# One stage in place of four: local attention and gated MLP of two layers in one pipeline, the softmax's exponential taken head by head

## The chip, the cores and the metric

The kernel runs on one core of a Trainium2 chip. The core has TensorE (PE; its weight loads are PEld), VectorE (DVE), ScalarE (ACT), GpSimd (POOL) and SyncE (SP, which only issues DMAs here). Each runs its own list of instructions in order, and they meet by semaphores. The metric is the device time of one execution in microseconds (us), median of several runs.

## The reference, cut to what matters

The kernel computes four sub-layers on x of 4 sequences, 1024 tokens, width 128. The change is in the last one, two layers of windowed attention with a gated MLP:

```python
def _layer(x, wqkv, qs, ksc, wo, lg, lb, w1, b1, w2, b2):
    h = shift_token(x)                  # the upper 64 features come from the token before
    q, k, v = split(h @ wqkv, 3)        # 8 heads of 64
    q = l2norm(q) * qs; k = l2norm(k) * ksc
    q, k = rotary_xpos(q, k)
    o = local_attention(q, k, v)        # windows of 64: own window and the one before, softmax
    x = x + o @ wo
    h = shift_token(x)
    h = (h - mean(h)) / sqrt(var(h) + 1e-05) * lg + lb
    a, g = split(h @ w1 + b1, 2)        # 341 each
    x = x + (a * gelu(g)) @ w2 + b2
    return x
```

A sequence of the second layer needs all its own tokens of the first, but nothing of the other sequences.

## The kernel before

`STAGES` (L1805) lists nine stages, one after the other, with a barrier of all engines between them. Activations lie with features on partitions and the 4096 tokens along the free dimension (`x`, `branch`). The last five stages are `normalise` (a layer norm of x into `branch`, which also loads the attention's weights), then `attend` and `gated_mlp` for each layer.

`attend` (L1326) works in tiles of 128 tokens, 32 tiles for a layer. It is software pipelined by hand: in step g an engine does the projection of tile g, the norm of tile g - 1 (`NORM`), the scores of g - 3 (`SCORE`), the exponential of g - 4 (`EXP`), the transposed probabilities and their product with the values for g - 5 (`VALUE`), and the output projection of g - 6 (`OUT`). `steps` (L52) writes the first steps out and loops over the rest. Within a step the order on each engine is the order of the code.

- TensorE: eight transposes of the turned q and k (L1377), three projections of 128x512 (L1389), eight transposes of probabilities (L1399), mask and scores (L1411, L1425, L1430), output projection (L1443), values (L1464).
- ScalarE: copies of q, k out of PSUM (L1493, L1495), one Exp over all eight heads, 128x1024, in place in SBUF (L1500), Ln and Exp of the norms (L1505, L1508), copies L1513, L1515, L1516 and L1521, a Square (L1528), the copy L1534. It also makes the shifted input `hs` (L1485, L1486).
- VectorE: sum of squares (L1590), floor (L1594), the rotary products (L1601, L1608), the sum of the exponentials (L1615), its reciprocal (L1618), the row maximum (L1624), scores less maximum from PSUM to SBUF (L1628), the add to `branch` (L1635), the other half of `v_mix` (L1638).
- GpSimd: three elementwise operations of 128x1024 (L1550, L1555, L1564).

`gated_mlp` (L1656) first runs `layer_norm` over all tokens, then goes in chunks of 512 tokens, eight for a layer: six matmuls up (L1713), three Gelu on ScalarE (L1745), three gated products on VectorE (L1766), three matmuls down (L1722), and the add (L1772). Gelu and Exp lie in different tables of ScalarE; `preload_act_table_set` loads one at the start of a stage. The store of the result is issued chunk by chunk by SP.

Every matmul here is float32, and the profile shows each as two records.

## Time and profile before

| | us |
|---|---|
| median of 3 runs | 1866.24 (1866.13 to 1867.06) |
| the profiled execution | 1866.51 |
| its span, first to last instruction | 1864.7 |
| `attend`, first layer | 1036.3 to 1350.1: 313.8 |
| `layer_norm` and `gated_mlp`, first layer | 1350.1 to 1449.7: 99.6 |
| `attend`, second layer | 1449.7 to 1763.3: 313.6 |
| `layer_norm` and `gated_mlp`, second layer | 1763.3 to 1864.7: 101.4 |

Over the span PE is busy 78%, DVE 71%, ACT 57%, POOL 49%. These are means over nine stages with different limits; the four stages in the lower half of the table hold 828.4 us. A row of the timeline gives start, duration, engine, line and operation, and in brackets the idle time before it and who ended it. A duration ends when the result is out; on ScalarE and TensorE the next instruction starts some 0.1 to 0.2 us earlier, so that what an instruction costs its engine is the distance of two starts.

### The profile page before, as it was taken

Reading aid. Unit: us, or ns where it says so; the run is one execution under the profiler, and the core shown is the slowest. Engines: PE = TensorE matmul, PEld = TensorE weight load, DVE = VectorE, ACT = ScalarE, POOL = GpSimd, SP = SyncE. Lnnn points to the kernel's source line nnn. Section 1 sums busy time; section 2 is a strip of 40 time slices with the busy share of each in tenths; the row PEclk is TensorE's granted clock in tenths of the full one; section 3 lists DMA queues with packets and bytes.
Section 4 is the critical chain, followed back from the end, with each engine's and each line's share of the span. In section 5 each row is a group of like instructions: output and inputs, shape, how many; then the busy total and the mean of one; then the engine's idle time right before and its main releaser. Section 6 shows DMA issues by size and latency. Waiting matters only on the chain. (4 is left out here: it accounts for less than half of the span.)

```text
span 1864.7 us, 26805 instructions
## 1 busy us (share of the span) xinstructions
PE 1445.9 (78%) x8740; PEld 800.6 (43%) x8740; DVE 1316.6 (71%) x1932; ACT 1061.9 (57%) x1849; POOL 917.2 (49%) x468
## 2 busy tenths in 40 slices
PE   6755299667577777777679689999789689999789
PEld 2314288323122223222233256666634366666533
DVE  2954133266799999999721699999633699999534
ACT  4431155487656666566444677887542587887442
POOL 0431433103888988888500277767400466776300
PEclk8875599887799999999989899999979899999989
DMA  1007111300000000000001000000010000000001
GB/s 58 0 6 158 58 46 34 91 0 1 0 1 1 0 1 0 0 0 0 0 12 48 3 1 2 0 0 0 1 61 0 1 2 2 0 0 0 13 6 40
DMA packets 35020, 30.08 MB, mean 16 GB/s; under 512 B 7763, under 2 KB 29573, under 8 KB 34566
## 3 DMA queue, kind: packets, MB, share of 16 engines
q1 hardware_dynamic: 32646, 24.48, 5.0%
q0 software_dynamic: 2304, 4.74, 0.8%
q8 instruction: 35, 0.57, 0.1%
q14 instruction: 35, 0.29, 0.1%
HBM read 19.73 MB, written 9.47 MB: 16 GB/s over the span
## 5 line engine op out<-in xcount | busy, mean ns | idle before, releaser
L1550 POOL TENSOR_TENSOR at_direct<-at_direct,at_square 128x1024 f32<-128x1024 f32 x64 | 152.5, 2383 | 412.4 <-DVE at_square L1608 412.4
L1023 POOL TENSOR_TENSOR ssm_dbu<-ssm_dtu,ssm_b_all 128x1024 f32<-128x1024 f32 x128 | 298.5, 2360 | 21.6 <-ACT ssm_b_all L976 21.1
L884 PE MATMUL ssm_bank<-ssm_seen,ident 128*128 128x512 f32 x512 | 247.4, 606 | 45.1 <-POOL ssm_seen L1031 37.7
L971 ACT ACTIVATE ssm_bank<-ssm_dt,ssm_decay 128x512 f32<-128x512 f32 x256 | 176.8, 691 | 118.0 <-DVE ssm_state L1122 115.6
L1389 PE MATMUL at_ps<-at_wqkv,at_hs 128*128 128x512 f32 x384 | 187.9, 628 | 32.8 <-ACT at_hs L1486 17.6
L1122 DVE TENSOR_TENSOR_SCAN ssm_state<-ssm_bank,ssm_dbu 128x512 f32<-128x512 f32 x128 | 147.9, 1204 | 15.4 <-POOL ssm_dbu L1023 15.1
L1122 DVE TENSOR_TENSOR_SCAN ssm_state<-ssm_bank,ssm_carry,ssm_dbu 128x512 f32<-128x512 f32 x128 | 155.3, 1263 | 1.9 <-POOL ssm_dbu L1023 1.6
L884 PEld LDWEIGHTS ssm_bank<-ssm_seen,ident 128*128 128x128 f32 x512 | 95.8, 193 | 131.0 <-issue 63.9
L1555 POOL TENSOR_TENSOR at_prob<-at_prob,at_inv 128x1024 f32<-128x1024 f32 x64 | 121.4, 1897 | 21.8 <-DVE at_inv L1618 21.8
L1564 POOL TENSOR_TENSOR at_direct<-at_direct,at_rnorm 128x1024 f32<-128x1024 f32 x64 | 131.4, 2053 | 0.5
L1389 PEld LDWEIGHTS at_ps<-at_wqkv,at_hs 128*128 128x128 f32 x384 | 71.4, 199 | 108.0 <-issue 75.9
L1130 DVE TENSOR_TENSOR ssm_seen<-ssm_state,ssm_bank 128x1024 f32<-128x1024 f32 x96 | 114.5, 1193 | 0.0
L871 PE MATMUL ssm_bank<-ssm_parts,ssm_pick 128*128 (+1 forms) x128 | 50.0, 391 | 73.6 <-DVE ssm_seen L1130 73.5
L976 ACT ACTIVATE ssm_b_all<-ssm_bank 128x512 f32<-128x512 f32 x128 | 74.7, 584 | 47.2 <-PE ssm_bank L862 26.7
L1443 PE MATMUL at_ps<-at_oT,at_wo 128*128 128x128 f32 x512 | 73.6, 287 | 32.5 <-ACT at_v_mix L1516 31.1
L1590 DVE TENSOR_REDUCE at_sums<-at_square 128x16 f32<-128x1024 f32 x64 | 78.0, 1219 | 22.6 <-ACT at_square L1528 21.0
L1031 POOL TENSOR_TENSOR ssm_seen<-ssm_state,ssm_c_all 128x1024 f32<-128x1024 f32 x32 | 75.2, 2350 | 34.5 <-ACT ssm_c_all L980 34.5
L1713 PE MATMUL glu_bank<-glu_normed,glu_w 128*128 (+3 forms) x192 | 90.5, 625 | 1.7 <-DVE glu_w L1758 1.7
L1608 DVE TENSOR_TENSOR at_square<-at_qk,at_turn 128x256 f32<-128x256 f32 x256 | 90.7, 411 | 0.0
L1745 ACT ACTIVATE glu_gelu<-glu_bank,glu_b 128x512 f32<-128x512 f32 (+1 forms) x48 | 32.9, 685 | 92.6 <-PE glu_bank L1713 92.6
L1615 DVE TENSOR_REDUCE at_total<-at_prob 128x8 f32<-128x1024 f32 x64 | 77.2, 1206 | 9.0 <-ACT at_prob L1500 9.0
L1601 DVE TENSOR_TENSOR at_direct<-at_qk,at_turn 128x512 f32<-128x512 f32 x128 | 81.9, 678 | 0.0
(240 smaller groups left out, 3418.0 us busy)
## 6 DMA issues: line engine op xcount, KB each, us to landing
moe_w<-in_moe_w SPq DMA_DIRECT2D x16, 256.0 KB
moe_to_experts<-moe_empty SPq DMA_DIRECT2D x10, 258.0 KB, 8.0
moe_slot_rows<-moe_to_experts SPq DMA_DIRECT2D x10, 258.0 KB, 3.0
x<-in_x SPq DMA_DIRECT2D x8, 256.0 KB, 3.4
moe_rows<-moe_from_experts SPq DMA_DIRECT2D x8, 256.0 KB, 4.5
at_turn<-in_turn SPq DMA_DIRECT2D x2, 1024.0 KB
out_x<-x SPq DMA_DIRECT2D x8, 256.0 KB, 2.0
at_wqkv<-in_wqkv SPq DMA_DIRECT2D x2, 768.0 KB
```

Source lines behind the costliest of these rows:

```text
L884: last = nc.tensor.matmul(bank[Y0 + half][:], ident[:], seen[:, n % 2, half], start=n == 0, stop=False)
L971: nc.scalar.activation(bank[DA0 + half][:], dt[:, half, cols(b * 2 + k)], ACT.Exp, scale=decay[:, half, n:n + 1]).then_inc(s[f"da{half}"], 1)
L1023: nc.gpsimd.tensor_tensor(dbu[:, n % RING], dtu[:, k], b_all[:, n % 2:n % 2 + 1, :].broadcast_to([P, 2, CH]), ALU.mult).then_inc(s["dbu"], 1)
L1122: nc.vector.tensor_tensor_scan(state[:, n % RING, half], bank[DA0 + half][:], dbu[:, n % RING, half], start, ALU.mult, ALU.add).then_inc(s ...
L1130: nc.vector.tensor_tensor(seen[:, n % 2], state[:, n % RING], bank[C0][:].unsqueeze(1).broadcast_to([P, 2, CH]), ALU.mult).then_inc(s["see ...
L1389: last = nc.tensor.matmul(ps[:, to], hs[:, i * TILE:(i + 1) * TILE], w[:, m * INNER:(m + 1) * INNER], start=True, stop=True)
L1550: nc.gpsimd.tensor_tensor(direct[:, quarter], direct[:, quarter], crossed[:, half], ALU.add).then_inc(s["added"], 1)
L1555: nc.gpsimd.tensor_tensor(prob[:, half], prob[:, half], inv[:, half].unsqueeze(2).broadcast_to([P, HEADS, TILE]), ALU.mult).then_inc(s["we ...
L1564: nc.gpsimd.tensor_tensor(heads, heads, rnorm[:, half].unsqueeze(2).broadcast_to([P, 2 * HEADS, HEAD]), ALU.mult).then_inc(s["scaled"], 1)
L1601: nc.vector.tensor_tensor(to, of, turn[:, 0, at_tile, m:m + 1].broadcast_to([P, HEADS, HEAD]), ALU.mult)
L1608: last = nc.vector.tensor_tensor(to[:, :, h0:h0 + 32], of[:, :, h1:h1 + 32], turn[:, 1, at_tile, m:m + 1, h0:h0 + 32].broadcast_to([P, HEA ...
L1713: last = nc.tensor.matmul(bank[3 * m + c][0:size, :], w1[:, m * HID + first:m * HID + first + size], normed[:, cols(t)], start=True, stop= ...
```

## The change

The four stages become one, `ffn`, with steps g = 0 to 76 (`LAST`) over the 64 tiles of both layers; nothing in it is a loop of the machine, every step is written out. The tile's pipeline keeps its lags. In addition each chunk c of 512 tokens, once its four tiles have gone through the attention, has its MLP spread over seven steps: `chunk_at(g, 0)` is true in step 9 + 4c. A step so carries pieces of two chunks. I call a step kind 0, 1, 2 or 3 by (g - 9) mod 4, and bare where it has no piece of an MLP:

- kind 0: first two `values` of the chunk before, the output projection of the chunk (`to_rows`, four matmuls of 512 columns for four tiles together, two before and two after the scores);
- kind 1: the third `values` and two `down` of the chunk before, `centring`, a Square on ScalarE;
- kind 2: the third `down`, `variance`, then Ln and Exp (`root`), the normalised chunk on VectorE;
- kind 3: three `gates` on TensorE, a table load, three Gelu and a table load back on ScalarE.

Softmax: VectorE takes the row maximum as before and multiplies it by -1 (`lowered`); ScalarE takes the exponential from PSUM in eight instructions of 128x128, one for each head, with the negated maximum as bias and the row sum as a second output (`accum_out`). The subtraction (L1628) and the sum (L1615) on VectorE go. The scores' PSUM banks are held until the exponentials are done.

The token shifts (`hs`, `hs2`) and both halves of `v_mix` are now DMAs from SBUF to SBUF, issued by SP. The sum x + branch is on GpSimd. `normalise` loads the weights of both layers, the MLP's too, in 36 DMAs where it had 11.

```diff
-                if live(EXP):
-                    n, half = g - EXP, (i - EXP) % 2
-                    act.wait_ge(s["shifted"], done(n))
-                    nc.scalar.activation(prob[:, half], prob[:, half], ACT.Exp).then_inc(s["prob"], 1)
...
+LAST = PER_CHUNK * (ALL_CHUNKS - 1) + FIRST + 7
+HELD = 6
+TURNED = 3
...
+        def chunk_at(g, step):
+            c, phase = divmod(g - FIRST - step, PER_CHUNK)
+            return c if phase == 0 and 0 <= c < ALL_CHUNKS else None
...
+            def shift(q):
+                for c in range(q * CHUNKS, (q + 1) * CHUNKS):
+                    k = c % CHUNKS
+                    of = chunk_of(branch, c)
+                    sp.dma_start(hs[0:64, q % 2, k * CH:(k + 1) * CH], of[0:64]).then_inc(s["hs"], 16)
+                    sp.dma_start(hs[64:128, q % 2, 1 + k * CH:1 + (k + 1) * CH], of[64:128]).then_inc(s["hs"], 16)
...
+                c = chunk_at(g, 0)
+                if c is not None:
+                    sp.wait_ge(s["attended"], up_to(c))
+                    k, q = c % CHUNKS, c // CHUNKS
+                    if q >= 2:
+                        sp.wait_ge(s["centred"], up_to((q - 1) * CHUNKS - 1))
+                    of = chunk_of(branch, c)
+                    sp.wait_ge(s["hs2"], 32 * c)
+                    sp.dma_start(hs2[0:64, q % 2, k * CH:(k + 1) * CH], of[0:64]).then_inc(s["hs2"], 16)
+                    sp.dma_start(hs2[64:128, q % 2, 1 + k * CH:1 + (k + 1) * CH], of[64:128]).then_inc(s["hs2"], 16)
+                if real(g) and not opens(g):
+                    sp.wait_ge(s["v_copied"], up_to(g))
+                    if real(g - HELD):
+                        sp.wait_ge(s["av"], up_to(g - HELD))
+                    if real(g - 2):
+                        sp.wait_ge(mixed[g % 2], mixes(g - 2))
+                    sp.dma_start(v_mix[0:64, g % HELD], v[0:64, g % HELD]).then_inc(mixed[g % 2], 16)
+                    sp.dma_start(v_mix[64:128, g % HELD], v[64:128, (g - 1) % HELD]).then_inc(mixed[g % 2], 16)
...
+            for g in range(LAST + 1):
+                n = g - SCORE
...
+                if chunk_at(g, 4) is not None:
+                    values(chunk_at(g, 4), (0, 1))
+                if chunk_at(g, 0) is not None:
+                    to_rows(chunk_at(g, 0), (0, 1))
+                if chunk_at(g, 5) is not None:
+                    values(chunk_at(g, 5), (2,))
+                if chunk_at(g, 6) is not None:
+                    down(chunk_at(g, 6), (2,))
+                if chunk_at(g, 2) is not None:
+                    variance(chunk_at(g, 2))
+                if chunk_at(g, 3) is not None:
+                    gates(chunk_at(g, 3))
...
+                    nc.tensor.matmul(one[:], at, wqkv[:, g // PER_LAYER, 2 * INNER:], start=True, stop=True
+                                     ).then_inc(s["v_proj"], 1)
+                    if real(n):
+                        pe.wait_ge(s["kT_copied"], up_to(n))
...
+                if chunk_at(g, 5) is not None:
+                    down(chunk_at(g, 5), (0, 1))
+                if chunk_at(g, 0) is not None:
+                    to_rows(chunk_at(g, 0), (2, 3))
+                if chunk_at(g, 1) is not None:
+                    centring(chunk_at(g, 1))
...
+            def gelus(c):
+                act.preload_act_table_set("gelu_and_others")
+                if c >= 1:
+                    act.wait_ge(s["down"], up_to(c - 1))
+                for p, (first, size) in enumerate(HID_PARTS):
+                    act.wait_ge(s["gates"], c * PARTS_OF_HID + p + 1)
+                    nc.scalar.activation(hidden[0:size, p], glu[PART_BANK[p]][0:size, :], ACT.Gelu,
+                                         bias=b1[0:size, c // LAYER_CHUNKS, 1, p:p + 1]).then_inc(s["gelu"], 1)
+                act.preload_act_table_set("natural_log_exp_and_others")
...
+                n = g - EXP
+                if real(n):
+                    act.wait_ge(s["lowered"], up_to(n))
+                    if real(n - 2):
+                        act.wait_ge(s["pT"], up_to(n - 2))
+                        act.wait_ge(s["inv"], up_to(n - 2))
+                    for h in range(HEADS):
+                        last = nc.scalar.activation(prob[:, n % 2, h],
+                                                    scores[:, h // 4, h % 4 * TILE:(h % 4 + 1) * TILE], ACT.Exp,
+                                                    bias=peak[:, n % 2, h:h + 1], accum_out=total[:, n % 2, h:h + 1])
+                    last.then_inc(s["prob"], 1)
...
+                c = chunk_at(g, 2)
+                if c is not None and c >= LAYER_CHUNKS:
+                    pool.wait_ge(s["attended"], up_to(c))
+                    nc.gpsimd.tensor_tensor(chunk_of(x, c), chunk_of(x, c), chunk_of(branch, c), ALU.add
+                                            ).then_inc(s["summed"], 1)
...
+            def prods(c, parts):
+                for p in parts:
+                    size = HID_PARTS[p][1]
+                    dve.wait_ge(s["gelu"], c * PARTS_OF_HID + p + 1)
+                    dve.wait_ge(s["values"], c * PARTS_OF_HID + p + 1)
+                    nc.vector.scalar_tensor_tensor(hidden[0:size, p], glu[VALUE_BANK[p]][0:size, :],
+                                                   b1[0:size, c // LAYER_CHUNKS, 0, p:p + 1], hidden[0:size, p],
+                                                   ALU.add, ALU.mult).then_inc(s["prod"], 1)
...
+                n = g - SCORE
+                if real(n):
+                    dve.wait_ge(s["sim"], up_to(n))
+                    of = scores[:].rearrange("p a (h j) -> p (a h) j", h=4)
+                    nc.vector.tensor_reduce(peak[:, n % 2], of, AX_X, ALU.max).then_inc(s["peak"], 1)
+                    dve.wait_ge(s["peak"], up_to(n))
+                    nc.vector.tensor_scalar(peak[:, n % 2], peak[:, n % 2], -1.0, None, ALU.mult
+                                            ).then_inc(s["lowered"], 1)
...
+STAGES = [min_gru, experts, mamba, mlp, normalise, ffn]
```

ScalarE, one step in the middle of the attention before; `at_ps` is PSUM, `at_prob` the probabilities of eight heads, `at_pT` their transposes, `at_oT` the attention's output of a tile:

```order
L1493 ACTIVATE at_qT<-at_ps 128x512
L1495 ACTIVATE at_kT<-at_ps 128x4x128
L1500 ACTIVATE at_prob<-at_prob 128x1024
L1505 ACTIVATE at_log<-at_floor 128x16
L1508 ACTIVATE at_rnorm<-at_log 128x16
L1511 REGISTER_ALU
L1513 ACTIVATE at_qk<-at_ps 128x1024
L1515 ACTIVATE at_v<-at_ps 128x512
L1516 ACTIVATE at_v_mix<-at_ps 64x512
L1521 ACTIVATE at_pT<-at_ps 128x1024
L1528 ACTIVATE at_square<-at_qk 128x1024
L1534 ACTIVATE at_oT<-at_ps 128x512
```

The same engine now, a step of kind 3; `at_one`, `at_two` and `at_scores` are the PSUM banks that `at_ps` was, `at_total` the sums, `at_hidden` the gate of the MLP:

```order
L1705 ACTIVATE at_oT<-at_one 128x4x128
L1712 ACTIVATE at_qT<-at_two 128x512
L1717 ACTIVATE at_kT<-at_two 128x4x128
L1728 ACTIVATE at_prob,at_total<-at_scores,at_peak 128x128 x8
L1738 ACTIVATE at_v<-at_one 128x512
L1689 ACT_TABLE_LOAD
L1694 ACTIVATE at_hidden<-glu_bank,ffn_b 128x512 x2
L1694 ACTIVATE at_hidden<-glu_bank,ffn_b 85x512
L1696 ACT_TABLE_LOAD
L1747 ACTIVATE at_log<-at_floor 128x16
L1752 ACTIVATE at_rnorm<-at_log 128x16
L1758 ACTIVATE at_qk<-at_two 128x1024
```

After that follow the square (L1763) and the copy of the transposed probabilities (L1769). One exponential became eight, the copy L1516 is gone, v is copied ahead of q and k, and in one step of four the Gelus stand between the copies.

TensorE, a step before (the rest of the scores, in the same alternation, is left out):

```order
L1377 MATMUL at_ps<-ident,at_direct 128x128 x8
L1382 REGISTER_ALU
L1389 MATMUL at_ps<-at_wqkv,at_hs 128x512 x3
L1399 MATMUL at_ps<-ident,at_prob 128x128 x8
L1411 MATMUL at_ps<-at_mask,at_eye 128x512 x2
```

And now, the first half of a step of kind 1 and, from the transposed probabilities on, its second half:

```order
L1555 MATMUL at_two<-ident,at_direct 128x128 x8
L1515 MATMUL glu_bank<-at_normed,ffn_w 85x512
L1580 MATMUL at_one<-ffn_wqkv,at_hs 128x512
L1587 MATMUL at_two<-ffn_wqkv,at_hs 128x512 x2
L1598 MATMUL at_scores<-ffn_mask,ffn_eye 128x512 x2
```

```order
L1638 MATMUL at_two<-ident,at_prob 128x128 x8
L1539 MATMUL glu_bank<-at_hidden,ffn_w 128x512 x2
L1504 MATMUL glu_bank<-at_hs,centre 128x512
L1670 MATMUL at_one<-at_pT,at_v_mix 64x64 x2
L1670 MATMUL at_one<-at_pT,at_v 64x64 x2
```

The scores now stand ahead of the transposed probabilities, which go into the same banks `at_two` as the transposes of q and k and the projections of q and k, so these three take turns; matmuls of the MLP (`glu_bank`) stand between them.

## Rows read from the trace of the kernel before

**Rows 1.** Busy us by stage; columns: stretch, us, PE, PEld, DVE, ACT, POOL, clock, DMA, GB/s:

```profile
1036.30:1350.10 313.80, 271.53 (x3072) 189.34 (x3072) 283.60 (x449) 229.76 (x369) 200.24 (x96) 0.97 0.00 1
1350.10:1449.70 99.60, 86.77 (x188) 36.80 (x188) 37.01 (x61) 32.91 (x50) 0.00 (x0) 0.90 0.09 29
1036.30:1864.70 828.40, 716.23 (x6520) 452.42 (x6520) 646.73 (x1028) 525.27 (x838) 400.46 (x192) 0.95 0.02 7
```

**Rows 2.** Timeline of PE, a step of the attention; columns: start, us, engine, line, operation:

```profile
1180.87 0.34 PE L1464 MATMUL at_ps<-at_pT,at_v_mix 128*64 128x64 f32 x4
...
1181.95 1.10 PE L1377 MATMUL at_ps<-ident,at_direct 128*128 128x128 f32 x8
1182.88 2.74 PE L1389 MATMUL at_ps<-at_wqkv,at_hs 128*128 128x512 f32 x6
1185.46 1.04 PE L1399 MATMUL at_ps<-ident,at_prob 128*128 128x128 f32 x8
1186.33 0.59 PE L1411 MATMUL at_ps<-at_mask,at_eye 128*128 128x512 bf16 x2
...
1187.69 0.27 PE L1425 MATMUL at_ps<-at_kT,at_qT 64*64 64x128 f32 x1
```

**Rows 3.** Timeline of ACT, the same step:

```profile
1183.92 0.60 ACT L1493 ACTIVATE at_qT<-at_ps 128x512 f32<-128x512 f32 x1
1184.41 0.59 ACT L1495 ACTIVATE at_kT<-at_ps 128x512 f32<-128x512 f32 x1
...
1185.99 0.20 ACT L1505 ACTIVATE at_log<-at_floor 128x16 f32<-128x16 f32 x1
1186.23 0.22 ACT L1508 ACTIVATE at_rnorm<-at_log 128x16 f32<-128x16 f32 x1
1186.37 1.02 ACT L1513 ACTIVATE at_qk<-at_ps 128x1024 f32<-128x1024 f32 x1
1187.29 0.59 ACT L1515 ACTIVATE at_v<-at_ps 128x512 f32<-128x512 f32 x1
1187.76 0.58 ACT L1516 ACTIVATE at_v_mix<-at_ps 64x512 f32<-64x512 f32 x1
```

**Rows 4.** Timeline, drain of the first attention: transposes, their copy, the values' matmuls:

```profile
1344.55 1.09 PE L1399 MATMUL at_ps<-ident,at_prob 128*128 128x128 f32 x8 [1.40 <-POOL at_prob L1555]
...
1345.68 1.02 ACT L1521 ACTIVATE at_pT<-at_ps 128x1024 f32<-128x1024 f32 x1 [1.89 <-PE at_ps L1399]
...
1346.76 0.34 PE L1464 MATMUL at_ps<-at_pT,at_v_mix 128*64 128x64 f32 x4 [0.22 <-ACT at_pT L1521]
```

**Rows 5.** ACT with a bias from SBUF; groups by line: count, busy us, mean ns:

```profile
L1745 ACT ACTIVATE glu_gelu<-glu_bank,glu_b 128x512 f32<-128x512 f32 x32 | 22.0, 687 | 76.1 <-PE glu_bank L1713 76.1
```

**Rows 6.** Timeline of ACT, one of its smallest operations and the next:

```profile
392.85 0.21 ACT L919 ACTIVATE ssm_dbu<-ssm_dbu 128x6 f32<-128x6 f32 x1
392.97 1.06 ACT L921 ACTIVATE ssm_dbu<-ssm_bank 128x512 f32<-128x512 f32 x2
```

**Rows 7.** Timeline of ACT, two loads of its table around one activation:

```profile
382.12 1.28 ACT L906 ACT_TABLE_LOAD   x1 [3.39 <-issue]
383.41 0.23 ACT L907 ACTIVATE ssm_decay<-ssm_a_log 128x32 f32<-128x32 f32 x1
383.66 1.28 ACT L908 ACT_TABLE_LOAD   x1
```

**Rows 8.** The line L1594: count, ns min/median/max, first and last start:

```profile
L1594 DVE TENSOR_SCALAR at_floor<-at_sums x64: 174/506/1596, 1048.3 to 1731.9; 128x16 f32<-128x16 f32 x64
```

**Rows 9.** Timeline of SP in `normalise`, its last three loads of eleven:

```profile
1019.76 1.66 SPq L132 DMA_DIRECT2D at_scales<-in_k_scale  x3
```

**Rows 10.** Waits of SP: us in total, times, longest:

```profile
SPq L107 <- DMA at_scales<-in_k_scale: 17.2, 2, 8.6
```

**Rows 11.** Timeline of PE, the first projections of the first attention:

```profile
1038.94 4.95 PE L1389 MATMUL at_ps<-at_wqkv,at_hs 128*128 128x512 f32 x6 [6.79 <-ACT at_hs L1486]
```

**Rows 12.** The last piece of the chain that ended last: start, us, what:

```profile
1861.02 0.69 DVE x L1776
```

More of the change, by code:

```diff
@@ new lines, in ffn @@
+        hidden = sb("hidden", [P, PARTS_OF_HID, CH])
+        two = ctx.enter_context(nc.psum_tensor("at_two", [P, 2, CH], F32))
+        scores = ctx.enter_context(nc.psum_tensor("at_scores", [P, 2, CH], F32))
+        one = ctx.enter_context(nc.psum_tensor("at_one", [P, CH], F32))
+        glu = [ctx.enter_context(nc.psum_tensor(f"glu_bank{n}", [P, CH], F32)) for n in range(3)]
+        PART_BANK = (1, 2, 0)
+        VALUE_BANK = (1, 2, 1)
+        s = dict(zip(FFN.split(), semaphores(ctx, nc, "ffn", FFN)))
@@ new lines, in _ @@
+            for layer in range(LAYERS):
+                for m in range(2):
+                    for p, (first, size) in enumerate(HID_PARTS):
+                        at = (layer * 2 + m) * PARTS_OF_HID + p
+                        last = nc.tensor.matmul(glu[0][0:size, at:at + 1],
+                                                w1[:, layer, m * HID + first:m * HID + first + size],
+                                                ln_b[:, layer:layer + 1], start=True, stop=True)
+            last.then_inc(s["lb_done"], 1)
@@ L1458, in step @@
                     for pair in range(4):
[L1459 removed]
+                        for q, values_of in ((0, v_mix), (1, v)):
                             for odd in range(2):
@@ L1462, in step @@
                                 to = slice(HEAD * odd, HEAD * odd + HEAD)
[L1463 to L1467 removed]
+                                at = pair * TILE + q * WINDOW
```

737 lines of the change are left out of this document (381 added, 356 removed).

## The prediction

> **What bounds the kernel now.** I read the busy table by stage first. The four stages that become one hold 828.4 us; the two MLP stages with their norms about 100 us each, the attentions 314 each. In an attention VectorE is busy 283.6 of 313.8 us, fill and drain of the pipeline included, so 283.6 / 32 = 8.86 us for a tile, and TensorE by its records 271.5 [rows 1]. In the MLP stage TensorE is busy 86.8 of 99.6 us and VectorE 37.0, ScalarE 32.9, GpSimd nothing [rows 1]. So one kind of stage waits for VectorE, the other for TensorE, and putting one under the other looks like a gain. What decides is whether the merged step is as short as the work of its busiest engine, and it isn't: the engines hand one PSUM pair back and forth. For that I read one step of TensorE and of ScalarE by starts.
>
> **Costs by starts.** TensorE, per step: eight transposes 1182.88 - 1181.95 = 0.93; three projections 1185.46 - 1182.88 = 2.58, so 0.86 for one float32 matmul of 512 columns; transposed probabilities 0.87; mask and scores about 1.5; the values' products 1181.95 - 1180.87 = 1.08 [rows 2]. ScalarE: a copy of 512 columns 0.49, Ln 0.24, Exp of the norms 0.14, the copy of q and k 0.92, v 0.47 [rows 3]. Handing over: from the first of eight transposes to the start of their copy 1.13, from that start to the first values' matmul 1.08 [rows 4]. Four transposes to the start of a copy I put at 0.66, half of 0.93 and the 0.2 by which 1.13 exceeds 0.93.
>
> **The eight exponentials** are the term that no row shows. A bias from SBUF makes a 512-column activation 0.687 [rows 5] where one without takes 0.60 [rows 3]. Two copies of 512 start 0.49 apart and one of 1024 takes 0.92, so a column costs 0.84 ns and one head 0.687 - 384 x 0.00084 = 0.365, of which 0.105 overlap with the next: 0.26 by starts. The second output costs nothing at best: 8 x 0.26 = 2.1 us. At worst the sum is read out by an instruction as long as the smallest, 0.21, after the full 0.365 [rows 6]: 8 x 0.575 = 4.6 us. I take one more small instruction in the stream, 0.12 by starts [rows 6]: 8 x 0.38 = 3.05 us. Call this E.
>
> **The step, walked.** Time 0 is the first transpose of q and k. TensorE and ScalarE wait for each other here: copies of q and k at 0.66 and 1.15; exponentials from 1.64 to 1.64 + E; v, Ln, Exp 0.85, so the copy of the new q and k starts at 2.5 + E. Its banks are free 1.07 later, the transposed probabilities follow, their copy starts 1.13 on, the values' matmuls 1.08 after that, and the next step's transposes another 1.08. Bare step: 6.86 + E = 9.91 us. Scores and mask lie in the gap behind the exponentials, which free their banks. ScalarE is never idle for more than 2 us in this, so the old 8.86 of VectorE is not what counts: VectorE's step falls by two operations of about 1.2 us and has slack. A step of each kind, from the same numbers:
>
> - kind 0: TensorE has 0.93 + 4 x 0.86 (two `values`, two `to_rows`) + 3 x 0.86 = 6.95 until the projections are issued, then 1.5 of scores, 0.87, two `to_rows` 1.72, 1.08: 12.1 us, and E is covered by it up to about 4.5;
> - kind 1: the bare step, 0.27 for a copy of the window's edge, and between transposed probabilities and values 3 x 0.86 = 2.58, of which 2.21 - 0.87 = 1.34 is hidden by the copy: 9.91 + 0.27 + 1.24 = 11.4;
> - kind 2: Ln and Exp of 512 columns, one after the other, 1.15: 11.1. Its two matmuls on TensorE lie under the exponentials;
> - kind 3: two table loads and three Gelu. A load ends 1.29 after it starts and the next activation follows 0.01 later [rows 7]; 2 x 1.3 + 3 x 0.6 + 0.1 = 4.5: 14.4. The three `gates`, 2.58, lie under the exponentials.
>
> That is 49.0 us for four steps, 12.25 for a tile, against (313.8 + 99.6) / 32 = 12.9 before [rows 1]. The gain in the steady part is 0.65 us for a tile, about 5%, far less than the busy times promise.
>
> **A rule against the table row.** The Trainium skill (ScalarE: Activation LUTs, What ACT_TABLE_LOAD costs) puts every switch of set at about 2.66 us, 1.28 for the load and 1.38 for a drain. The trace disagrees: load and next activation follow each other within 0.01 [rows 7]. With the page's figure, an estimate, kind 3 would be 2 x 1.38 = 2.8 longer and the stage, 16 times that, 44 us.
>
> **What lies off the path.** The small multiplication by -1 on VectorE is of the kind of the floor, which takes 174 ns alone and up to 1596 [rows 8] beside GpSimd. Here it comes some 7.5 us into a step and is wanted at 11.6 or later, so 1.6 us is covered; GpSimd's three operations, 200.2 / 32 = 6.3 us a tile [rows 1], fit too, with the extra add of x. The SBUF copies by SP are wanted a step or five later; a landing would have to take more than 4 us to show.
>
> **Start and end.** `normalise` now issues 36 loads instead of 11. Three took 1.66 us [rows 9], about 0.5 each, so the last goes out near 1016 + 18 = 1034 and lands, by the 8.6 us that SP waited for the last one before [rows 10], at 1042 at the latest; without a queue in front of it 2 us, 1036. I take a barrier at 1041.3, 5 us late. The first tile needs four shift DMAs and the edge: 4.5 us, so step 0 at 1045.8; the first matmuls run at half the clock, 4.95 us for three projections [rows 11]. Steps 0 to 4, without probabilities or with few: 26. Steps 5 to 8, bare: 4 x 9.9 = 40. Steps 9 to 63: 13 x 49.0 + 12.1 + 11.4 + 11.1 = 671.6, less 3 since the first chunk has none before it. Then the drain: steps 64 to 66 about 11.8, 9.8 and 10.6; 67 and 68 together 14; then one chunk's MLP alone as a chain: the rest of its output projection 5.2, add 0.7, shift DMA 2.6, centring 1.0, Square 0.6, variance 1.1, Ln and Exp 1.3, normalising 0.7, first gate 1.1, three Gelu, values, products and downs in each other's wake 8, add 0.75, store and end 3, as the 1864.7 - 1861.7 now [rows 12]; 25.8 in all, and 2 for a clock at half there. Sum of the drain 74. End: 1045.8 + 26 + 40 + 668.6 + 74 = 1854.4. The profiled execution lies 1.8 above its span and the median 0.3 below it: 1856, and 1 for small waits: **1857 us**, 0.5% below 1866.24.
>
> **The rivals.**
> - *The sum is read out only behind each finished exponential* (slower). A head is 0.365 + 0.12 = 0.49, E 3.9. It counts in kinds 1 to 3, bare steps and part of the drain, some 48 steps: +0.85 x 48 = 41, 1898; at the upper bound, 4.6, 1931. It decides from E = 3.25, a read-out of 0.145 us: above that the change loses. Against it: smallest operations start 0.12 apart. For it: a sum is only there after the last column.
> - *The second output is free* (E = 2.1): -0.95 x 48 = -46, 1811.
> - *ScalarE and TensorE overlap more than the walk has it*, if the copies start on less than I count: -0.5 in each of 64 steps, 1825.
> - *Waits the walk leaves out* (the DMAs, VectorE beside GpSimd), 0.4 in each of 64 steps: +25, 1882.
> - *TensorE's clock falls to its lower level* of 1.2 GHz. In the attentions before it was granted 0.97 [rows 1] with TensorE hardly idle; now it waits about 1 us at three places of a step. At the lower level a projection costs twice as much [rows 2, 11]; a step would be some 8 us longer. In a tenth of the steps: 1908.
> - *A table load in the middle of a full queue stalls about as long again as it lasts*: 1.28 twice in 16 chunks [rows 7], 41 us, 1898. The rows speak against it: the second load starts 0.02 after an activation ends and nothing follows it.
>
> The Trainium skill's figure for a switch, above, is what this last rival would look like; by it the sum would be 1901.
>
> **How the numbers follow.** Forecast 0.40, with 1840 to 1876 as its own range (E by 0.2 either way 10 us, start and drain 8); late read-out 0.24; free second output 0.12; more overlap 0.05; waits 0.09; clock 0.06; drain of the table 0.04. Below 0.2% is what a measurement of this kernel can't tell from no change. Of the forecast's 0.40, 0.29 lie more than 3.7 us under 1866.2, 0.08 within, 0.03 above. Faster 0.29 + 0.12 + 0.05 = 0.46, same 0.08, slower 0.03 + 0.24 + 0.09 + 0.06 + 0.04 = 0.46. The range leaves out half of the free output, the upper part of the late read-out and part of the clock: 1820 to 1912.
>
> **What would show it.** In the profile after: the exponentials' starts within a tile 0.38 apart (0.26 or 0.49 for the rivals); table load to next activation 1.3; bare steps of 9.9, a chunk's four steps of 49; TensorE idle before the transposed probabilities until the copy of q and k; the clock at 1.0 from step 5 to 63; VectorE idle for a quarter of a step or more; the first projection about 7 us later than 1038.94. Wrong would be the whole picture if VectorE or GpSimd were what TensorE and ScalarE wait for, or if the steps of kind 3 were no longer than the others.

## The result, and the profile after

The changed kernel takes 1924.06 us (1923.48 to 1925.15) against 1866.18 us of the kernel before on the same chip: the ratio is 1.031, with a 95% interval of 1.0293 to 1.0328. The forecast was 1857 in a range of 1820 to 1912. The change loses 58 us, and lies 67 us above the forecast and outside its range. The profiled execution took 1924.02, its span is 1922.2, and that is what the readings below are made against. Every median below is of executions in the faster state, but for one of the eight of the kernel before beside the second four experiments, which took 4301.29 us (without it their median is 1867.75 and not 1868.2).

The page of after, parts 1, 2 and 4:

```profile
PE 1476.3 (77%) x8356; PEld 791.9 (41%) x8356; DVE 1129.9 (59%) x1718; ACT 1178.5 (61%) x2756; POOL 921.4 (48%) x476
...
PEclk8875699786999999999897898899989999998999
...
PE 32%; ACT 6%; issue 4%; DVE 2%; DMA 1%; SPq 1%; DVEq 0%
```

No engine is busier than 77%; before, none was above 78%. The digits of the clock from slice 23 on (the merged stage) mix 8 and 9 all the way, with one 7, where full speed would read 9 throughout. The busy table for the stretch from 1100 to 1905, and for one step of kind 3, in the columns of [rows 1]:

```profile
1100.00:1905.00 805.00, 691.52 (x5882) 415.06 (x5882) 411.73 (x745) 606.00 (x1668) 378.29 (x189) 0.93 0.13 29
```

```profile
1213.90:1230.40 16.50, 12.00 (x95) 7.81 (x94) 7.17 (x16) 12.91 (x31) 7.16 (x4) 0.78 0.00 1
```

Starts of the copy of q mark the steps. Their medians are 13.6 us for kind 0, 11.4 for kind 1, 10.8 for kind 2, 16.5 for kind 3 and 9.7 for a bare step. The forecast had 12.1, 11.4, 11.1, 14.4 and 9.9. So two kinds and the bare step came as walked, and kinds 3 and 0 are 2.1 and 1.5 too long. The second row is a step of kind 3, and its clock is 0.78 where the attention before had 0.97 [rows 1].

The timeline of PE of after, from a step of kind 3 into kind 0:

```profile
1319.21 2.74 PE L1515 MATMUL glu_bank<-at_normed,ffn_w 128*128 128x512 f32 x6
...
1324.37 0.59 PE L1598 MATMUL at_scores<-ffn_mask,ffn_eye 128*128 128x512 bf16 x2
...
1329.38 1.94 PE L1638 MATMUL at_two<-ident,at_prob 128*128 128x128 f32 x8 [3.38 <-issue]
...
1332.43 0.48 PE L1670 MATMUL at_one<-at_pT,at_v_mix 128*64 128x64 f32 x4 [1.11 <-ACT at_pT L1769]
...
1334.34 1.75 PE L1555 MATMUL at_two<-ident,at_direct 128*128 128x128 f32 x8
1335.92 1.45 PE L1515 MATMUL glu_bank<-at_normed,ffn_w 128*128 128x512 f32 x3
```

and the busy table over the same stretch, in slices:

```profile
1322.00:1325.00 3.00, 3.00 (x12) 1.07 (x14) 0.20 (x1) 2.97 (x9) 2.85 (x2) 1.00 0.00 0
1325.00:1328.00 3.00, 1.00 (x32) 0.75 (x32) 1.39 (x2) 2.97 (x5) 0.07 (x1) 1.00 0.00 0
1328.00:1330.00 2.00, 0.62 (x3) 0.65 (x4) 0.00 (x0) 1.94 (x4) 1.49 (x1) 0.73 0.00 0
1330.00:1332.00 2.00, 1.32 (x7) 0.92 (x5) 1.56 (x3) 1.01 (x2) 0.41 (x1) 0.50 0.03 8
1332.00:1334.00 2.00, 1.57 (x30) 1.57 (x32) 2.00 (x6) 0.38 (x1) 0.00 (x0) 0.50 0.00 0
1334.00:1336.00 2.00, 2.00 (x17) 1.88 (x15) 0.37 (x2) 1.11 (x2) 1.55 (x1) 0.57 0.00 0
1336.00:1338.00 2.00, 2.00 (x6) 0.88 (x6) 0.00 (x0) 1.96 (x11) 0.80 (x1) 1.00 0.01 4
```

TensorE has finished the scores at 1326 and waits 3.38 us. From 1329 to 1335.9 the granted clock is 0.50, the lower of its levels (1.2 GHz). What it does then stands on the path: the transposed probabilities take 1.94 against 1.04 [rows 2], the 32 small matmuls of the values start over 1.91 us against 1.08 [rows 2], the next transposes over 1.58 against 0.93 [rows 2]. That is 0.9 + 0.8 + 0.65, and with the first `values` matmul (L1515) behind them some 2.5 us or more in each chunk, thirteen times up to step 60.

What it waited for is on ScalarE; the timeline of ACT of after in the same step:

```profile
1325.35 1.25 ACT L1694 ACTIVATE at_hidden<-glu_bank,ffn_b 128x512 f32<-128x512 f32 x2
1326.61 1.28 ACT L1696 ACT_TABLE_LOAD   x1
1327.91 0.22 ACT L1747 ACTIVATE at_log<-at_floor 128x16 f32<-128x16 f32 x1
1328.15 0.21 ACT L1752 ACTIVATE at_rnorm<-at_log 128x16 f32<-128x16 f32 x1
1328.28 1.01 ACT L1758 ACTIVATE at_qk<-at_two 128x1024 f32<-128x1024 f32 x1
```

The copy of q and k, which frees the banks of the transposed probabilities, comes behind eight exponentials, three Gelu and two table loads. From load to next activation it is 1.30 us, as in [rows 7].

The eight exponentials, from the timeline of ACT of after:

```profile
1309.11 0.37 ACT L1728 ACTIVATE at_prob<-at_scores,at_peak 128x128 f32<-128x128 f32 x1
1309.36 0.21 ACT L1728 ACTIVATION_READ_ACCUMULATOR at_prob<-at_scores,at_peak 128x1 f32 x1
1309.45 0.38 ACT L1728 ACTIVATE at_prob<-at_scores,at_peak 128x128 f32<-128x128 f32 x1
...
1311.85 0.66 ACT L1738 ACTIVATE at_v<-at_one 128x512 f32<-128x512 f32 x1
```

The second output is an instruction of its own. A read-out starts 0.25 us behind its exponential, and the next exponential 0.09 behind the read-out, so a head costs 0.34 and eight of them 1311.85 - 1309.11 = 2.74 us.

### The profile page after: what moved, and what is told of

Same layout as the page of the kernel before. It is cut to its first block and busy times, and to the rows that moved or that the text cites. A ratio compares the mean times of both kernels' runs of the same rounds, so it can differ in the third digit from the quotient of the medians.

```text
span 1922.2 us, 26306 instructions
## 1 busy us (share of the span) xinstructions
PE 1476.3 (77%) x8356; PEld 791.9 (41%) x8356; DVE 1129.9 (59%) x1718; ACT 1178.5 (61%) x2756; POOL 921.4 (48%) x476
## 3 DMA queue, kind: packets, MB, share of 16 engines
q1 hardware_dynamic: 46438, 47.46, 10.1%
## 5 line engine op out<-in xcount | busy, mean ns | idle before, releaser
L1728 ACT ACTIVATE at_prob<-at_scores,at_peak 128x128 f32<-128x128 f32 x512 | 180.5, 396 | 1.8 <-DVE at_peak L1900 1.8
L1790 POOL TENSOR_TENSOR at_prob<-at_prob,at_inv 128x1024 f32<-128x1024 f32 x64 | 121.5, 1898 | 81.4 <-DVE at_inv L1884 81.4
L1898 DVE TENSOR_REDUCE at_peak<-at_scores 128x8 f32<-128x1024 f32 x64 | 78.3, 1224 | 122.6 <-PE at_scores L1617 112.2
L1796 POOL TENSOR_TENSOR at_direct<-at_direct,at_rnorm 128x1024 f32<-128x1024 f32 x64 | 124.1, 1940 | 51.0 <-ACT at_rnorm L1752 50.7
L1587 PE MATMUL at_two<-ffn_wqkv,at_hs 128*128 128x512 f32 x256 | 124.6, 610 | 1.7 <-ACT at_qk L1758 1.4
L1884 DVE RECIPROCAL at_inv<-at_total 128x8 f32<-128x8 f32 x64 | 12.9, 202 | 192.1 <-ACT at_prob L1728 192.1
L1638 PE MATMUL at_two<-ident,at_prob 128*128 128x128 f32 x512 | 78.8, 304 | 56.5 <-issue 45.5
L1728 ACT ACTIVATION_READ_ACCUMULATOR at_prob<-at_scores,at_peak 128x1 f32 x512 | 121.1, 236 | 0.0
L1670 PE MATMUL at_one<-at_pT,at_v_mix 128*64 128x64 f32 x896 | 69.8, 255 | 41.7 <-ACT at_pT L1769 41.7
L1515 PE MATMUL glu_bank<-at_normed,ffn_w 128*128 128x512 f32 (+1 forms) x192 | 100.0, 648 | 2.1 <-DVE at_normed L1913 2.1
L1705 ACT ACTIVATE at_oT<-at_one 128x512 f32<-128x512 f32 x64 | 38.4, 600 | 98.7 <-PE at_one L1670 98.7
```

Of the source, the lines that this page charges most:

```text
L1515: return nc.tensor.matmul(glu[to][0:size, :], w1[:, c // LAYER_CHUNKS, m * HID + first:m * HID + first + size], normed[:], start=True, sto ...
L1587: last = nc.tensor.matmul(two[:, half], at, wqkv[:, g // PER_LAYER, half * INNER:(half + 1) * INNER], start=True, stop=True)
L1638: last = nc.tensor.transpose(two[:, h // 4, (h % 4) * TILE:(h % 4 + 1) * TILE], prob[:, n % 2, h], ident[:])
L1670: last = nc.tensor.matmul(one[to, at:at + WINDOW], values_of[:, n % HELD, h * HEAD:(h + 1) * HEAD], pT[:, pair + 4 * odd, q * WINDOW:(q + ...
L1728: last = nc.scalar.activation(prob[:, n % 2, h], scores[:, h // 4, h % 4 * TILE:(h % 4 + 1) * TILE], ACT.Exp, bias=peak[:, n % 2, h:h + 1] ...
L1790: nc.gpsimd.tensor_tensor(prob[:, m % 2], prob[:, m % 2], inv[:, m % 2].unsqueeze(2).broadcast_to([P, HEADS, TILE]), ALU.mult).then_inc(s[ ...
```

## The experiments

Steps are named by their kind. The experiments ran in three groups, and the kernel before, measured beside each on the same chip, took 1865.22 us with the first four (filler, values early, one exponential, no read-out), 1868.2 with the next four (both, late loads, no table loads, before by head) and 1864.59 with the last two. Ratios are to it. So a difference of two medians from different groups, or from after, is good to about 4 us. The traces differ besides in when the loads in front of the merged stage start, from 1011.5 to 1019.1, which no edit touches; steps 9 to 63 are free of that.

### Fill the wait of kind 3

```diff
                     last.then_inc(s["sim"], 1)
+                if chunk_at(g, 3) is not None and real(g):
+                    pe.wait_ge(s["v_copied"], up_to(g))
+                    for _ in range(3):
+                        nc.tensor.matmul(one[:], centre[:], wqkv[:, 0, 0:CH], start=True, stop=True)
                 n = g - VALUE
```

> The changed kernel with three matmuls of 512 columns added on TensorE in every step of kind 3, between the scores and the transposed probabilities, into the bank that v has left; their product is overwritten. TensorE then idles about 0.8 us there instead of 3.4. Theory, the clock: the granted clock stays at 1.0, so transposed probabilities, values' products, the next transposes and the two values of the MLP, some 3.3 us a chunk, come at full speed: 1924 - 15 x 3.3 = 1874. Rival, the wait itself is all there is: added work in a gap changes nothing, 1922 to 1926.

1887.12 us, ratio 1.0118 (1.0101 to 1.0135): 37 us less than after, with more work. The timeline of PE:

```profile
1420.12 2.84 PE L1631 MATMUL at_one<-ffn_wqkv,centre 128*128 128x512 f32 x6
1423.58 1.07 PE L1642 MATMUL at_two<-ident,at_prob 128*128 128x128 f32 x8 [0.61 <-issue]
1425.76 0.34 PE L1674 MATMUL at_one<-at_pT,at_v_mix 128*64 128x64 f32 x4 [1.11 <-ACT at_pT L1773]
```

The wait for the copy is as long as before, only 2.6 us of it are filled. The transposes are back at 1.07. Kind 3 is 14.35 us in seven of thirteen chunks, the forecast's 14.4, and 14.55 to 15.9 in the others; kind 0 is 12.3 and 13.35 by turns in most. Matmuls that nobody reads can't shorten any chain of data, so these 37 us are the clock's: 2.8 for each of the thirteen steps that hold the filler. The theory had counted fifteen at 3.3 us. The profiled execution, 1893.26, is the longest of the four (the others took 1886.4 to 1887.2), and steps 9 to 63 are 29.4 us shorter in it than in after.

### Useful work in the same wait

```diff
-                if chunk_at(g, 4) is not None:
-                    values(chunk_at(g, 4), (0, 1))
...
                     last.then_inc(s["sim"], 1)
+                if chunk_at(g, 3) is not None:
+                    values(chunk_at(g, 3), (0, 1))
                 n = g - VALUE
```

> The first two values matmuls of a chunk are moved from the start of kind 0 into the gap of kind 3, right behind the scores; nothing is added. Theory, clock and TensorE's share in kind 0 together: 3.3 + 1.7 us a chunk, 1924 - 15 x 5 = 1849. If only kind 0 gets shorter and the clock matters nothing: 1898. If kind 0 waits for ScalarE and not for TensorE: 1924.

1859.97 us, ratio 0.9979 (0.9969 to 0.9989): 64 us less than after, more than the lesser theory's 1898 and near the 1849 of the two together. Kind 3 is 14.36, kind 0 is 10.6 and 11.6 by turns. Against the kernel with the filler it gains 27 us, and two matmuls of 512 columns less in kind 0, 2 x 0.86 for each of fifteen chunks, are 26. So the 64 us are about 37 of clock and 27 of work moved into a wait. The clock is 0.99 over the whole steady part:

```profile
1100.00:1830.00 730.00, 644.45 (x5830) 375.34 (x5828) 413.32 (x741) 599.51 (x1662) 376.22 (x188) 0.99 0.14 32
```

### One part alone: the merged stage with the softmax of before

```diff
-                    act.wait_ge(s["lowered"], up_to(n))
...
-                    for h in range(HEADS):
...
+                    act.wait_ge(s["shifted"], up_to(n))
+                    nc.scalar.activation(prob[:, n % 2], prob[:, n % 2], ACT.Exp).then_inc(s["prob"], 1)
...
+                    nc.vector.tensor_reduce(total[:, n % 2], prob[:, n % 2], AX_X, ALU.add).then_inc(s["total"], 1)
...
-                    nc.vector.tensor_scalar(peak[:, n % 2], peak[:, n % 2], -1.0, None, ALU.mult
-                                            ).then_inc(s["lowered"], 1)
+                    nc.vector.tensor_tensor(prob[:, n % 2], of,
+                                            peak[:, n % 2].unsqueeze(2).broadcast_to([P, HEADS, TILE]),
+                                            ALU.subtract).then_inc(s["shifted"], 1)
```

> The merged stage with the softmax as it was before: VectorE subtracts the maximum and sums, ScalarE takes one exponential of 128x1024. Theory, the eight exponentials are on the path: ScalarE's step falls by 2.74 - 0.95 = 1.8 us, VectorE's rises by 2.4 to some 8.9, so kinds 1 to 3 and the bare steps fall by about 1.3: 1924 - 47 x 1.3 = 1862. Rival, taking work off VectorE was what the merge needed: VectorE's longer chain from scores to exponential gives all of it back, 1924 or more.

1892.68 us, ratio 1.0153 (1.0137 to 1.017). Between the two expectations: in the merged stage the softmax by head costs 31 us, and merging costs 27 without it. Kinds 1 and 2 are 10.6 and 10.1, kind 0 is 13.9 and 15.0 by turns, kind 3 15.6 and 16.5, and the clock over the steady part is 0.93 as in after. With the MLP's pieces in the order of after, the clock falls with either softmax. (With the `values` early it is otherwise, see below.)

### The other part alone: the stages of before with the softmax by head

```diff
-                    act.wait_ge(s["shifted"], done(n))
-                    nc.scalar.activation(prob[:, half], prob[:, half], ACT.Exp).then_inc(s["prob"], 1)
+                    act.wait_ge(s["lowered"], done(n))
...
+                    for h in range(HEADS):
+                        last = nc.scalar.activation(prob[:, half, h],
+                                                    ps[:, SIM + h // 4, h % 4 * TILE:(h % 4 + 1) * TILE], ACT.Exp,
+                                                    bias=peak[:, half, h:h + 1], accum_out=total[:, half, h:h + 1])
...
-                    nc.vector.tensor_reduce(total[:, half], prob[:, half], AX_X, ALU.add).then_inc(s["total"], 1)
```

> The kernel before, four stages, with the softmax by head alone: eight exponentials from PSUM with bias and sum, no subtraction and no sum on VectorE. VectorE's 8.9 us a tile fall to about 7, ScalarE's rise by 1.8 to 8.6. Theory, ScalarE is then just under the old bound: 1845 to 1866. Rival, scores held for longer make TensorE and ScalarE wait in turn, as in the merged stage: a tile of 9.9, 1866 + 64 x 1 = 1930.

1928.96 us, ratio 1.0321 (1.0302 to 1.034): the rival was right in its sum. A step of the attention is 9.5 us, where it was 8.9. The timeline of ACT, over one such step:

```profile
1235.06 0.60 ACT L1540 ACTIVATE at_oT<-at_ps 128x512 f32<-128x512 f32 x1 [0.49 <-PE at_ps L1464]
1236.07 0.60 ACT L1493 ACTIVATE at_qT<-at_ps 128x512 f32<-128x512 f32 x1 [0.42 <-PE at_ps L1377]
1236.57 0.59 ACT L1495 ACTIVATE at_kT<-at_ps 128x512 f32<-128x512 f32 x1
1237.04 0.37 ACT L1503 ACTIVATE at_prob<-at_ps,at_peak 128x128 f32<-128x128 f32 x1
...
1239.79 0.27 ACT L1511 ACTIVATE at_log<-at_floor 128x16 f32<-128x16 f32 x1
...
1244.55 0.60 ACT L1540 ACTIVATE at_oT<-at_ps 128x512 f32<-128x512 f32 x1 [0.49 <-PE at_ps L1464]
```

Two waits of 0.49 and 0.42 are all that ScalarE has left in 9.5 us; the exponentials take 2.75 of it, from 1237.04 to 1239.79. The clock is 1.00 between 1217 and 1255, so it plays no part in this. The edit takes two operations of 1.2 us from VectorE, which was the busiest, and fills ScalarE by starts to 8.6 us a step, as the theory had it. The step is 0.9 longer than that, since ScalarE waits for TensorE, and TensorE for ScalarE. The waits of TensorE over four steps, 1217 to 1255 (us in total, times, longest):

```profile
PE at_ps L1443 <- ACT at_v_mix L1522: 2.5, 4, 0.6
PE at_ps L1411 <- ACT at_prob L1503: 2.1, 4, 0.5
```

So the two wait in turn, as the rival said, but in a step of 9.5 and not 9.9, and 64 times 0.6 is only 38 of the 61 us. More lies at the edges of the sequences, where steps of 9.35 and 7.78 us are now 10.49 and 9.63, and in fill and drain. That the rival's 1930 came out so closely is in part luck. Without the merge the softmax by head costs 61 us, more than the whole change.

### The read-out of the sums

```diff
-                                                    bias=peak[:, n % 2, h:h + 1], accum_out=total[:, n % 2, h:h + 1])
+                                                    bias=peak[:, n % 2, h:h + 1])
```

> The eight exponentials without their second output; the sums are set to 1 once, so the softmax is not normalised. Theory, the read-out costs 0.09 us by starts and lies on the path: 8 x 0.09 x 47 steps = 34 us, 1890. Rival, it is hidden behind TensorE: 1924.

1900.23 us, ratio 1.0182 (1.0164 to 1.0199): 24 us less, where 34 was expected. Kinds 1 and 2 and the bare steps fall by 0.73, to 10.6, 10.1 and 9.0, which is eight times 0.09. The gain is not had in the other two: between steps 9 and 63 kinds 1 and 2 give 24 us and kind 3 gives 5, but kind 0 takes 10 back; the drain gives 4. The granted clock is 0.92 there, so it still falls in each chunk.

### No table loads

```diff
-                act.preload_act_table_set("gelu_and_others")
...
-                    nc.scalar.activation(hidden[0:size, p], glu[PART_BANK[p]][0:size, :], ACT.Gelu,
+                    nc.scalar.activation(hidden[0:size, p], glu[PART_BANK[p]][0:size, :], ACT.Relu,
...
-                act.preload_act_table_set("natural_log_exp_and_others")
```

> The changed kernel with Relu for Gelu and without the two table loads of each chunk. Theory, kind 3 loses 2.6 us of loads, and since TensorE's wait there falls from 3.4 to about 0.9 us, the half clock and its 3.3 us as well: 1924 - 16 x 2.6 - 15 x 2.5 = 1845. If only the loads count: 1882. If the loads carried a hidden drain of 1.3 us each too: 1924 - 83 or less.

1846.99 us, ratio 0.9883 (0.9866 to 0.9901): 77 us less. Kind 3 is 11.5 now. With the filler it was 14.35, and the 2.8 between them are two loads of 1.3 and a little. The rest is the clock, 0.99 between 1100 and 1800, the wait of kind 3 being shorter by the two loads. Of the 77 us the 32 loads are 42; 35 are left, about what the filler gave.

### Both: values early and one exponential

It is the edit of the second experiment on top of that of the third.

> Both edits of the runs before in one kernel: the first two values matmuls in the gap of kind 3, and one exponential over eight heads with VectorE's subtraction and sum. Theory, the two are independent: kinds 1 and 2 as in the run with one exponential, 10.6 and 10.1 us, kind 3 about 1 below the 14.4 of the run with early values, kind 0 at 11: 1860 - 31 - 10 = 1820. Rival, with TensorE quick again VectorE becomes the bound and most of the second edit is lost: 1850.

1842.4 us, ratio 0.9862 (0.9845 to 0.9878), nearer to the rival, but not for its reason. The bare steps are 8.5, kinds 1 and 2 10.6 and 10.1, as the theory had them, and in steps 9 to 63 no wait of TensorE or ScalarE is put down to VectorE. What is missing is elsewhere. Of the thirteen steps of kind 3 up to step 60 only four are 14.36 us, the others 15.2 to 15.65, and kind 0 is up to 12.4: in this kernel waits of 1.47 and 1.11 us behind the two `values` come with a clock that falls, as in this row of the busy table behind such waits:

```profile
1222.00:1224.00 2.00, 2.00 (x24) 1.88 (x23) 1.97 (x6) 0.60 (x1) 0.00 (x0) 0.53 0.00 0
```

### The start: less to load before the barrier

```diff
+            later = attend_loads(mem, dram, 1)[1]
+            for to, of in later:
+                sp.dma_start(to, of).then_inc(s["late"], 16)
...
+                    if g == PER_LAYER:
+                        pe.wait_ge(s["late"], 16 * len(attend_loads(mem, dram, 1)[1]))
...
-                if g == 2:
-                    tables(1)
-                    fold()
+                if g == 6:
+                    fold()
+                if g == 14:
+                    dve.wait_ge(s["late"], 16 * len(attend_loads(mem, dram, 1)[1]))
+                    tables(1)
```

Here `attend_loads` returns the small loads and, second, the twelve of weights and tables that the second layer alone needs. It stands on top of the kernel above.

> The same, and 12 of the 36 loads (second layer's wqkv, wo, turn, scales, w2) are issued inside the merged stage behind the first shift instead of in normalise; VectorE folds the norm's scale in step 6 and turns the second table in step 14 instead of both in step 2. Theory, the stage's start is late by its loads and step 2 by VectorE: barrier 6 to 7 us earlier, 4 us saved in steps 2 and 3: 10 us under the kernel without this edit. Rival, the loads compete with the shifts and v_mix copies: no gain.

1825.39 us, ratio 0.9777 (0.976 to 0.9794): 17 us less where 10 was expected. The timeline of SP shows the shift DMAs, the first thing behind the barrier, ten us earlier than in after (1046.36):

```profile
1036.27 0.53 SPq L1435 DMA_DIRECT2D at_hs<-branch  x1
```

Step 9 starts at 1112.5 instead of 1131.6. Of these 19 us, 2.6 lie ahead of the first load (1016.48 against 1019.08) and are not the edit's. From the first load to the barrier it is 19.7 us instead of 30.7, so 11 where the theory had 6 to 7, and from the barrier to step 9 it is 76.4 instead of 81.8, so 5 where it had 4.

### One more matmul in the wait

```diff
                     values(chunk_at(g, 3), (0, 1))
+                    if real(g):
+                        pe.wait_ge(s["v_copied"], up_to(g))
+                        nc.tensor.matmul(one[:], centre[:], wqkv[:, 0, 0:CH], start=True, stop=True)
```

> One exponential of 1024 columns, the two `values` early, the second layer's loads late (1825 us), and behind the two `values` of each step of kind 3 one more matmul of 512 columns whose result nobody reads, into the bank that the copy of v has left. In the kernel without it TensorE still waits 1.47 us there before the transposed probabilities and 1.11 us before the values' products, and in ten of sixteen chunks it comes out of these waits at 0.53 of its clock: kind 3 then lasts 15.3 to 15.6 instead of 14.36 us and kind 0 up to 12.3 instead of 10.6. Theory (what is left of the clock's fall hangs on those two waits, so 0.86 us of work in one of them lifts it): kinds 3 and 0 at 14.4 and 10.6 to 11.6 throughout, 15 us less, 1810. Rival (the fall has another cause, or another wait in the chunk is enough for it): 1825 or a little more.

1810.68 us, ratio 0.9712 (0.9696 to 0.9728), the fastest here, 2.9% under the kernel before. The timeline of PE:

```profile
1283.48 1.98 PE L1518 MATMUL glu_bank<-at_normed,ffn_w 128*128 128x512 f32 x4
1285.30 1.02 PE L1635 MATMUL at_one<-ffn_wqkv,centre 128*128 128x512 f32 x2
1286.94 1.06 PE L1646 MATMUL at_two<-ident,at_prob 128*128 128x128 f32 x8 [0.61 <-issue]
1289.12 0.34 PE L1678 MATMUL at_one<-at_pT,at_v_mix 128*64 128x64 f32 x4 [1.11 <-ACT at_pT L1770]
```

Kind 3 is 14.36 in all chunks but two. The medians differ by 15 us, the theory's figure, but the matmul doesn't give all of that. The two come from different groups, and by the ratios it is 12. In the traces steps 9 to 63 are 632.4 us against 642.5, so 10 less, and 1.5 are in the drain. The first load of this execution was issued 5 us earlier than in the kernel without the matmul (1016.48), which a matmul in kind 3 can't do:

```profile
1011.55 0.33 SPq L132 DMA_DIRECT2D ffn_wqkv<-in_wqkv  x1
```

So a matmul of 0.86 us whose result is thrown away gives 10 to 12 us.

### The change with both edits

The softmax by head, with the two `values` early and the late loads.

> The change as it is, with the softmax by head and its second output, but with the two `values` moved into the gap and twelve of the second layer's loads after the barrier. The first edit alone gave 1860, the second took 17 us from the kernel with one exponential. Theory (the start is a term of its own, independent of the softmax): 1843, so about 18 above the same kernel with one exponential. Rival (the late start hides behind something else here, since VectorE is less busy): 1855 to 1860.

1847.22 us, ratio 0.9907 (0.9883 to 0.9931): 4 above the theory's 1843, and 22 above the same kernel with one exponential. Against the kernel with the `values` early alone it is 13 less, where 17 was expected, so the start is nearly a term of its own. The softmax by head is not what it takes to beat the kernel before; it costs here too.

## Why the prediction was wrong

By the prediction's own sum the span should have ended at 1854.4; it ended at 1922.2. Of these 67.8 us, 16 came by step 9 (1128.5 against 1112.5), 44.9 in steps 9 to 63 (713.5 against 668.6), 6.9 in the drain (80.2 against 73.3).

**The step that failed is the clock.** The prediction took every duration on TensorE from a stretch at 0.97 and kept the fall to 1.2 GHz as a rival with a chance of 0.06, "in a tenth of the steps". Its own walk had what speaks against that. In kind 3 it counted 0.93 + 2.58 + 2.58 + 1.5 + 0.87 + 1.08 = 9.5 us of work for TensorE in a step of 14.4, so nearly 5 us idle, in the same place of each chunk. It named TensorE's idling before the transposed probabilities as a sign, but gave that gap no length: it spoke of "about 1 us at three places", and measured are 3.38 and 1.11. The clock fell not now and then but in every chunk, for 7 to 10 us each time. The price was not far off, 51 us there and 37 by the filler; the chance was. Before, the nearest case stood in [rows 11], a start behind a wait of 6.79 us at half the clock.

**Kind 0** was mis-sized besides. Without the table loads, where the clock holds, it is 12.3 and 13.35 by turns against 12.1. The longer ones hold the opening tile of a sequence, whose products with the values are of another shape (below): seven times 1.0 us up to step 63. The 44.9 us add up so: kind 3 is 27 over the walk in all, which is gone where the clock holds (14.36); kind 0 is 20 over, 8 of it the clock's (its fourteen steps hold 186.5 us against 178.0 without the table loads) and 12 its own size; kinds 1 and 2 are 2 under. So 35 are the clock's and 12 kind 0's.

**E** was taken at 3.05 and is 2.74. "One more small instruction in the stream" was right, and its price was 0.09 by starts, not 0.12. The rival of the late read-out, at 0.49 a head, is refuted: the heads start 0.34 apart. So is the free second output: without the read-out the time falls by 24 us. Kinds 1 and 2 and the bare step followed the walk within 0.3 us. With E at 2.74 the walk would give 9.6, 11.1, 10.8 and 14.1 for the bare step and kinds 1, 2 and 3, where 9.7, 11.4, 10.8 and, at full clock, 14.36 were measured: an E too long by 0.3 hid two terms too short by as much.

**The table load** was right at 1.3, and the rival of a stall with it. The page ScalarE: Activation LUTs of the Trainium skill (What ACT_TABLE_LOAD costs) would have each switch at 2.66 us. Here the next activation comes 1.30 after the load's start, with the queue full, and two loads less shorten kind 3 by 2.8 us. The trace disagrees with the page; the prediction rightly followed the row.

**The start** was 5 us late at the barrier and 11 more up to step 9. The 36 loads took longer to issue than at 0.5 each, a single one 3.42 us and three of the scales 2.66, so the last went out at 1038.65 and not 1034. The timeline of after, first around the barrier, then DVE in step 2:

```profile
1026.24 3.42 SPq L132 DMA_DIRECT2D ffn_turn<-in_turn  x1
...
1034.57 2.66 SPq L132 DMA_DIRECT2D ffn_scales<-in_q_scale  x3
1037.27 1.38 SPq L132 DMA_DIRECT2D ffn_scales<-in_k_scale  x3
...
1046.24 0.06 DVE L1807 MEMSET at_hs<- 64x2 f32 x1 [12.91 <-PEq L1931]
```

```profile
1068.87 4.50 DVE L1812 TENSOR_TENSOR ffn_turn<-ffn_turn,ffn_scales 128x1024 f32<-128x1024 f32 x2
1073.29 0.47 DVE L1821 TENSOR_TENSOR ffn_b<-ffn_b,glu_bank 128x2 f32<-128x2 f32 x6
1073.68 2.29 DVE L1824 TENSOR_SCALAR ffn_w<-ffn_w,ffn_ln_g 128x682 f32<-128x682 f32 x2
1075.90 1.21 DVE L1852 TENSOR_REDUCE at_sums<-at_square 128x16 f32<-128x1024 f32 x1
```

The prediction named no work of VectorE in the first steps. Nearly all of the 11 us lie ahead of step 5. The tables of the second layer and the folding of the norm's weights stand there in front of the sum of squares in step 2, 7 us, of which moving them to later steps gave 5 back. The rest of the 11 is not traced to one cause. The kernel with late loads has both terms out of the way and gains 17 us.

**The drain**, 7 us too long, runs partly at half the clock: transposes of 1.97 us at 1872.47. No experiment singles out that share. The softmax by head is in it too: the drain is 80.2 us against 69.8 with one exponential, and 76.8 against 68.0 with the `values` early.

**What was covered.** The multiplication by -1 takes 648 ns in the mean, and ScalarE waited 1.8 us in all for it. VectorE (411.7 busy of 805) is not what TensorE and ScalarE wait for in steps 9 to 63, as forecast, and GpSimd hardly is. TensorE waits for GpSimd's weighted probabilities in the thirteen steps of kind 2 from step 15 on (us in total, times, longest):

```profile
PE at_two L1638 <- POOL at_prob L1790: 9.5, 13, 0.7
```

**The sign** was an even chance by the prediction. The forecast gain was 9 us, and the clock was not needed to undo it: with the filler the kernel still takes 1887.12, since the start (16 us), kind 0 (12) and the drain (7) are each terms of about that size. What the shares of busy time hide is this: merging can be worth 54 us (1810.68 against 1864.59, with the softmax of before and three edits), and the softmax by head costs 18 to 31 in the merged stage (1859.97 against 1842.4, 1847.22 against 1825.39, 1924.06 against 1892.68) and 61 outside it, since ScalarE is in the chain of hand-overs in both. The 18 and 22 are small because the kernels with one exponential lose some clock in these two pairs.

**Open.** The kernel with `values` early and by head has the same two waits of TensorE, 1.5 us behind scores and `values` and 1.1 behind, as the one with one exponential, yet keeps its clock (0.99, and kind 3 at 14.36 in eleven of thirteen chunks), and the other loses it in nine steps of thirteen. The steps of the first are longer and TensorE is less filled in them. Why the same waits do different things is not settled, and with it not how long a wait in this kernel may be before the clock falls.

## What to carry to other kernels

When a merge is costed by walking a step, write down the gaps of TensorE too, not only the step's length, and look for one that recurs in each round; then fill it with work that is due soon, and price the matmuls behind it at half the clock until it is filled; here waits of 3.4 us cost the clock in every chunk, and waits of 1.5 and 1.1 in one kernel and not in another. An exponential taken by head with its sum as second output saves VectorE two passes but puts 2.7 us in small instructions where one of 1024 columns takes 1.1; in none of the four pairs here did it pay, and ScalarE is in the chain in all of them. Loads and set-up for a later layer belong behind the barrier, and behind the first steps.

## What the hardware showed that was not expected

- The sum of an activation is read out by a second instruction, which the page counts apart (the costliest groups of after):

```profile
L1728 ACT ACTIVATION_READ_ACCUMULATOR at_prob<-at_scores,at_peak 128x1 f32 x512 | 121.1, 236 | 0.0
```

Its record is 236 ns in the mean, but the next exponential starts 0.09 us behind it.

- Small matmuls were slower where they changed between 64 and 128 rows. In the timeline of PE of the fastest kernel, the products with the values of a sequence's opening tile:

```profile
1345.37 0.33 PE L1673 MATMUL at_one<-at_pT,at_v 64*64 64x64 f32 x4
1345.63 0.34 PE L1678 MATMUL at_one<-at_pT,at_v 128*64 128x64 f32 x4
...
1347.48 1.09 PE L1558 MATMUL at_two<-ident,at_direct 128*128 128x128 f32 x8
```

32 records in 2.11 us, where a tile that isn't the first has its 32 in 1.08 [rows 2]. Half of the records have 64 rows; whether the 64 rows or the change between the two makes them slower, no run separates.

- From the end of a wait of 3.38 us TensorE ran at 1.2 GHz for about 7 us; work in the wait that nobody needs made the kernel 37 us faster, and one matmul of 0.86 us in a shorter wait 10 to 12.
- Two VectorE multiplications of 128x1024 from SBUF took 2.36 us when alone and 4.50 beside GpSimd's operations (1046.37 and 1068.87 in after).
